# TensorE kept at work from the end of the projections into the attention loop

## The reference

```python
q_in = linear(x, Wq_w, Wq_b).transpose(0, 2, 1)
Q3 = conv1d(q_in, convq_w, convq_b, (1, 1))                  # 3 taps
Q = linear(concat([q_in, Q3]), qproj_w, qproj_b)             # heads; K the same way
V = linear(x, Wv_w, Wv_b)
tau   = sigmoid(conv1x1(gelu(depthwise_conv3(x))))           # (b, h, l), delta the same way
scores = einsum('bhqd,bhkd->bhqk', Q, K) / sqrt(DK)
scores = scores * tau[..., None] + delta[:, :, None, :]
out = linear(einsum('bhqk,bhkd->bhqd', softmax(scores), V), out_w, out_b)
x = layernorm(x + out)
x = layernorm(x + einsum('bsd,od->bso', mxfp4_quant(x), mxfp4_quant(weight)) + bias)
```

## Time and profile before

| what | value |
|---|---|
| runs | 1662.35 us (1661.26 to 1664.51) |
| profiled execution | 1652.92 us, span 1651.1 us |
| TensorE busy with matmuls | 1603.3 us, 97% of the span |
| VectorE busy | 1528.7 us, 93% |
| ScalarE busy | 1311.1 us, 79% |
| mean granted clock of TensorE | 0.991 |

### The profile page before, as it was taken

One profiled execution on the slowest core, in us unless ns is written; L12 is line 12 of the kernel. 1 busy time (PEld: TensorE's weight loads), 2 busy tenths in 40 slices (PEclk: granted clock), 3 DMA queues, 4 the chain that ended last, 5 costly groups with the idle time before them and its releaser, 6 DMA issues.

```text
span 1651.1 us, 34599 instructions
## 1 busy us (share of the span) xinstructions
PE 1603.3 (97%) x13839; PEld 716.9 (43%) x13844; DVE 1528.7 (93%) x1616; ACT 1311.1 (79%) x2375; POOL 448.0 (27%) x1189
## 2 busy tenths in 40 slices
PE   8999999999999999999999999999999999999986
PEld 7767763333333333333333333333333343433465
DVE  5789887999999999999999999999999999988887
ACT  2876837888888888888888888888888877778645
POOL 4222246222222222222222222222232222331200
PEclk9999998999999999999999999999999999999999
DMA  3376427000700060015003400432152001000312
GB/s 114 108 182 157 142 82 113 8 8 9 87 8 8 19 76 8 15 25 70 8 9 37 60 8 9 49 48 56 37 63 32 8 8 43 25 27 20 115 60 90
DMA packets 55385, 84.79 MB, mean 51 GB/s; under 512 B 14524, under 2 KB 25404, under 8 KB 53852
## 3 DMA queue, kind: packets, MB, share of 16 engines
q1 hardware_dynamic: 53368, 82.49, 24.3%
q10 hardware_dynamic: 1856, 0.09, 0.1%
HBM read 51.36 MB, written 30.67 MB: 50 GB/s over the span
## 4 chain that ended last, share of the span: by engine, by line
PE 67%; DVE 14%; ACT 2%; issue 2%; ACTq 0%; DVEq 0%
PE ps L918 30%; PE ps L905 23%; PE ps L227 12%; DVE mx L237 10%; PE ps L864 1%; ACT e L1048 1%; ACT ev L1037 1%; DVE stats L1149 1%; PE ps L862 1%; DVE work L1208 0%; DVE work L1197 0%; DVE small L1192 0%; PE ps L861 0%; DVE work L1205 0%; DVE xq L1211 0%
## 5 line engine op out<-in xcount | busy, mean ns | idle before, releaser
L237 DVE TENSOR_REDUCE mx<-ps 128x2 f32<-128x1024 f32 x1024 | 1239.1, 1223 | 49.7 <-PE ps L227 36.9
L1048 ACT ACTIVATE e<-ps 128x512 f32<-128x512 f32 x2048 | 1109.0, 596 | 207.6 <-PE ps L905 167.0
L918 PE MATMUL ps<-e,v_grp 128*32 128x256 f32 x8192 | 655.8, 392 | 5.8 <-ACT ev L1037 5.8
L905 PE MATMUL ps<-q,k 52*128 52x512 f32 x2048 | 525.6, 500 | 4.5 <-PEq L355 4.3
L227 PE MATMUL ps<-k,q 50*128 50x512 f32 x2048 | 414.5, 399 | 4.5 <-DVE mx L237 3.9
L248 POOL TENSOR_SCALAR mn<-mx 128x1 f32<-128x1 f32 x512 | 180.5, 359 | 847.4 <-DVE mx L237 847.1
L905 PEld LDWEIGHTS ps<-q,k 52*128 52x128 f32 x2048 | 200.0, 184 | 430.7 <-ACT e L1048 388.0
L918 PEld LDWEIGHTS ps<-e,v_grp 128*32 128x32 f32 x8192 | 161.7, 108 | 377.7 <-issue 202.7
L227 PEld LDWEIGHTS ps<-k,q 50*128 50x128 f32 x2048 | 196.8, 187 | 18.4 <-DVE mx L237 10.3
L251 POOL TENSOR_SCALAR nm<-mn,mx 128x1 f32<-128x1 f32 x512 | 141.7, 289 | 25.2
L681 PE MATMUL ps<-x_p,m_p 128*128 128x512 f32 x576 | 142.6, 402 | 0.0
(11 more groups left out here) (138 smaller groups left out, 611.6 us busy)
## 6 DMA issues: line engine op xcount, KB each, us to landing
k<-k_parts SPq DMA_DIRECT2D x42, 256.0 KB
q<-q_parts SPq DMA_DIRECT2D x84, 128.0 KB
k_parts<-k_sp SPq DMA_DIRECT2D x16, 512.0 KB, 4.9
q_parts<-q_sp SPq DMA_DIRECT2D x16, 512.0 KB, 4.1
att<-ev SPq DMA_DIRECT2D x32, 256.0 KB
x_c<-in_x_t SPq DMA_DIRECT2D x8, 514.0 KB, 5.8
tau_r<-tau_rows SPq DMA_DIRECT2D x16, 256.0 KB
q<-nm_rows SPq DMA_DIRECT2D x256, 2.0 KB
```

Source lines behind the costliest of these rows:

```text
L237: nc.vector.tensor_reduce(mx[:, j % 2, :, jh, qt, kc], ps[:, b0:b0 + 2, :], AX.X, ALU.max).then_inc(s_free, 1)
L905: nc.tensor.matmul(ps[:, st_bank(n), :], k_set[r, g % 2, jh, kt * P:(kt + 1) * P], q_set[r, g % 2, i % NQ, jh, :], start=True, stop=True). ...
L918: last = nc.tensor.matmul(ps[32 * h:32 * (h + 1), 0, PVW * part:PVW * (part + 1)], v_grp[:, kt, h, :], e[:, x % E_BUFS, h * CH + PVW * par ...
L1048: nc.scalar.activation(e[:, x % E_BUFS, h * CH:(h + 1) * CH], ps[:, st_bank(n), :], ACT.Exp).then_inc(e_ready, 1)
```

## The change

TensorE's stream gets 16 matmuls at the end of the first block and 12 between the loop's first scores whose result is never read (`unread`): they have the form of one half of a score unit and write banks that are free there (0 and 1, after `q_evac`; in the loop bank 0, which the first `pv_half` starts afresh). For the last chunk `values(7, 1)` and its `v_bias` go behind the last projection and the last `q_scale`. One more place (14) of the last chunk gets two units, whose maxima VectorE takes in the second block (`MAX_FROM` = `PRE` - 2, `PRE` now 44). Two more units are issued before the loop, one behind each key tile's scores.

```diff
+        def unread(bank, half):
+
+            r = rows_of(half, K_S)
+            nc.tensor.matmul(ps[:, bank, :], q_set[r, 0, 0, 0, 0:P], k_set[r, 0, 0, 0:CH], start=True, stop=True)
...
-        PRE_STEP = {2: PAIR_AT(10, 14)} | {n: PAIR_AT(6, 10, 14) for n in range(3, 7)} | {7: PAIR_AT(0, 2, 4, 6, 8, 10, 12)}
+        PRE_STEP = {2: PAIR_AT(10, 14)} | {n: PAIR_AT(6, 10, 14) for n in range(3, 7)} | {7: PAIR_AT(0, 2, 4, 6, 8, 10, 12, 14)}
...
+        MAX_FROM = PRE - PRE_STEP[NCHUNK - 1][-1]
...
                     pre_max(n, 3)
-                    v_bias(n, 1)
+                    if more:
+                        v_bias(n, 1)
                     pre_max(n, 4)
...
                     q_scale(n, 1)
-                    pre_max(n, 6)
+                    if more:
+                        pre_max(n, 6)
+                    else:
+                        v_bias(n, 1)
...
-                    values(n, 1)
+                    if n + 1 < NCHUNK:
+                        values(n, 1)
                     pre_scores(n, 10)
                     pe.wait_ge(k_split, CT * n + 2)
                     project(n, 0, 1, q_full, 11)
                     if n + 1 < NCHUNK:
                         pointwise(n + 1)
+                    else:
+                        values(n, 1)
                     pre_scores(n, 14)
+                pe.wait_ge(q_evac, CT * NCHUNK)
+                for _ in range(8):
+                    for half in range(2):
+                        unread(half, half)
...
+                    issued = PRE
                     for x in range(AHEAD):
                         for jh in range(HH):
                             st(x, jh)
-                    issued = PRE
+                            for _ in range(4 if x == 0 else 2):
+                                unread(0, 0)
+                            if jh == 1:
+                                s_item(issued)
+                                issued += 1
...
-                    run_items(PRE, w_first)
+                    run_items(MAX_FROM, w_first)
```

## The result

The changed kernel takes 1649.64 us (median of 11 runs, 1647.78 to 1654.95), the kernel before 1658.77 us (11 runs, the three shown above among them): a ratio of 0.9946, 95% interval 0.9928 to 0.9964. A second sample of both gave 1653.53 us (12 runs) against 1660.48 us (35 runs), ratio 0.9962 (0.9941 to 0.9984). One of those 35 runs, 1675.61 us, counts as slow and is left out of the ratio. The gain is some 6 to 9 us, where 5.3 was forecast, and the time lies under the stated range.

A forecast was written before the change was run, and what follows sets the result against it. TensorE, busy 39.75 us of each loop iteration of 39.99 to 40.00, was taken as the bound. +0.2 us at the first values product and -5.5 in the first iteration gave -5.3: 1657.0 us, range 1654.8 to 1660.8.

The forecast's parts named there:

- That the clock would stay up: End of the first block into the loop: TensorE's granted clock stays 1.00 from 240 to 300 us.
- A: Rival: the clock falls all the same, at the block's end or in the start-up; +1.4 us, 1663.8 us; chance 0.10.
- B: Rival: the clock falls there and stays down for more than four slots; slower, some 1666.5 us; chance 0.05.
- The loop's start: Change from first block to loop: the loop starts at 248.8 us instead of 249.76, 0.9 us earlier.
- The start-up: First score to first values product in the loop: 5.3 us with the unread matmuls, instead of 4.13 us.
- C: Rival: an unread matmul's weight load isn't hidden on one half, 0.19 us more each; gain 3.3 us, 1659.0 us; chance 0.05.
- Four pairs: First loop iteration: 32 score pairs to issue instead of 36, so four slots with two pairs go, 2.28 us less.
- The four slots at half clock: First iteration, 253.89 to 262.05 us: with the clock kept up, four slots take 5.0 instead of 8.16 us.
- I carry a difference in us over unchanged: Whole kernel: the gain summed on the profiled execution, 1652.92 us, is subtracted unchanged from the runs' median, 1662.35 us.
- What is late next is TensorE itself: First iteration after the change: no other engine delays it; TensorE sets the pace at 1.25 us a slot.
- The lead carried to the end: From the second iteration on nothing differs, so the whole lead of 5.3 us lasts to the end.
- D: Rival: the lead is lost in the late iterations, half of it, -2.6 us remaining, 1659.7 us; chance 0.07.

## Why the prediction was wrong

- **That the clock would stay up**: right, in both profiles of the changed kernel. A and B did not happen.
- **The loop's start**: forecast 0.9 us earlier. From the last chunk's first projection to the loop's first score it is 30.55 us in the profile before and 29.62 after, 0.93 less. The second pair of place 10 waited as worked out, and the unread pairs went at (2.01 - 0.39) / 7 = 0.23 us. Right.
- **The start-up**: forecast 5.3 us, measured 4.58. The four on one half took 1.08 us for four, (1.08 - 0.39) / 3 = 0.23 us from start to start, under 0.25: the load hides, and C is out. The rule of the Trainium skill weighed there (TensorE: Matmul & The Clock Gate, Part 3, packing small matmuls) does not hold for these matmuls. The 0.02 us less for each of twelve matmuls are 0.24 of the 0.7 us by which the start-up came out shorter than forecast; the rest is not taken apart.
- **Four pairs**: right; iteration 0 has 32, and no slot issues two. By the four slots (1.82, 1.81, 1.82 and 1.83 us before, 1.24, 1.24, 1.24 and 1.56 after) they are worth 2.0 us, where 2.28 was forecast.
- **The four slots at half clock, 3.16 us**: the term that was mis-sized. It is right for the profile that it was read from; over six profiles iteration 0 is 2.8 us longer than there, so the term is some 6.0 us on average. The sentence that failed is "I carry a difference in us over unchanged". The profiled execution was 9.43 us under the median of three runs (5.85 us under that of eleven), and the prediction stated it without asking what the slower runs had more of. Some 2.8 us of it was this half clock, that is, what the change removes; half clock elsewhere, 17.6 us there and 23.8 in the mean of six, went the same way.
- **"What is late next is TensorE itself"**: wrong, a wait put at nothing. GpSimd's folds were late, 2.0 us in the first profile, 1.5 in the second. The trace of before had the warning: 23.83 us of GpSimd work in iteration 0 against 11.25 in the next, and the wait of 6.6 us for the bias loads ahead of it.
- **The lead carried to the end** (D): nothing contradicts it. From iteration 1 to 25 both kernels take 1003 to 1005 us in every profile; iterations 26 to 31 take 277.0 to 282.6 us in either.

The sum by the steps as measured: -0.93 at the loop's start, +0.45 in the start-up, and iteration 0 from 48.26 (six profiles) to 42.0 (two), -6.26: -6.7 us, inside both intervals of the ratio (6.0 to 11.9 us and 2.7 to 9.8 us). By the one profile it would have been -3.9, less than the 5.3 forecast: the wait for GpSimd took more than the shorter start-up gave.

Of the 7.4 us between 1657.0 and 1649.64, 3.6 are the kernel before, whose median is 1658.77 with more runs than three, and 3.8 are the gain.

What stays open: why the same program stays at half clock for 13.7 us in one execution and 30.7 in another, while TensorE works without a pause. The length goes with the point of the gap at which the clock falls (six profiles, above), but no run here moves that point by itself.

## What to carry to other kernels

When the profiled execution is faster than the median of the runs, ask what the slower ones have more of before you carry a difference over: a mean clock per run, beside its time, shows it. A stretch of half clock is worth its average length, not the one in the profile. And an engine with slack on average (GpSimd, 27%) can be the next wait in the one iteration in which its extra work lies.

## What was not expected of the hardware

At half clock TensorE worked through the loop's slots without a pause for up to 24.90 us before the clock came back, at 2.16 us a slot instead of 1.24; in the execution that the prediction read it came back after 7.5 us of them. Single-half matmuls in a row went as fast as whole-array ones, 0.23 us each at 512 columns, with a weight load each, where the projections' took 0.25 us.
